# Second experts' down products with the weights stationary, copied out and turned back per token

## The chip, the cores and the metric

The kernel runs on one core of a Trainium2 chip. Its time is device microseconds for one execution; the runs before gave 628.49 us as the median of three (626.14 to 630.59). The trace comes from one further execution, which took 630.66 us.

## The reference

The program is a small language model tower on 16 x 128 tokens: a token layer with four MLP levels (width 128), an attention layer with a fast-weight recurrence (8 heads of 32), a first expert layer (8 experts, two chosen per sequence), a second attention layer, and a second expert layer (8 experts, two chosen per token). The change touches the last of these, and by one condition the first expert layer. Cut to what matters, the second expert layer is:

```
logits = xn @ Wr + br                       # xn: normalised x, 64 wide; 8 experts
top_vals, top_idx = top_k(logits, 2)
w_full = scatter(softmax(top_vals))         # 2 of 8 weights per token are not zero
for e in range(8):
    h = gelu(xn @ W1[e] + b1[e])            # 64 -> 128
    y_e = h @ W2[e] + b2[e]                 # 128 -> 64
    y = y + y_e * w_full[..., e, None]
return x + y
```

All eight experts are computed for every token, and the weights pick afterwards. All arithmetic is in float32.

## The kernel before

Five queues run by orders written out by hand: TensorE, VectorE, ScalarE, GpSimd and the DMA queue of SyncE. Each takes its instructions strictly in the order written, and waits on semaphores where it needs another engine's work. In the expert layers a "token" t is a block of 128 tokens (16 blocks), and four blocks make a chunk of 512 columns (c = 0 to 3). `x = 4 * k + c` numbers the chunks of both expert layers (k = 0, 1).

The steps of the second expert layer (k = 1), for one chunk:

- `turn_x` (L1567): four TensorE transposes of the normalised input into one PSUM bank. ScalarE's `experts` (L1054) copies it out with the norm's scale and bias.
- `expert_up` (L1583): for each expert one product of 512 columns with a contraction of 64 rows. Experts of even and odd number use different halves of the rows of the array. The result, 128 x 512, fills a PSUM bank; `expert_bank` (L367) names it. ScalarE's `expert_gelus` (L1067) takes it out through gelu into `G2`, of which there are two, for chunks of even and odd number.
- `expert_down` (L1617): for each block of 128 tokens eight products, one per expert. The stationary operand is the gelu block (128 x 128), the moving one the expert's weights (128 x 64). All eight fill one bank with tokens on the partitions and (expert, output) along the row (L1635). Banks 4 and 5 take turns.
- VectorE's `weigh` (L2503) multiplies that bank by the token's eight router weights into one of four buffers `ytmp`. GpSimd (L827 to L835) adds up the experts of two blocks in three halving additions and adds the sum to `H`; the last pair is done by VectorE (L2538 to L2543). SyncE sends `H` out in five transfers.

Beside it run the router of the second layer (`router`, `router_read`, `beaten_by`, `half_gaps`, `router_tanh`, `router_weights`), in two halves of eight blocks, and the experts' bias: the router's weights are turned (`turn_weights` L1814), saved by ScalarE (`save_weights` L1184) and multiplied by the biases (`second_bias` L1820, bank 7), and VectorE adds the result to `H` (`add_bias` L2497).

The order on TensorE around the change is L1830 to L1867, on ScalarE L1194 to L1211, on VectorE L2512 to L2543. On TensorE all down products of a chunk stand in few blocks: those of chunk 0 between the ups of chunk 1, those of chunk 1 between the ups of chunks 2 and 3, those of chunks 2 and 3 one after the other at the end. An up product waits for the gelu that freed its bank (`i >= 6`, L1588); four banks are in use.

The first expert layer (k = 0) has the same `expert_up`. In its chunk 0 experts 4 and 5 write to banks 4 and 5, which nothing else holds. Its down products have the router's weights multiplied into the expert weights, which stand still, 64 wide, while 128 gelu columns move; the experts of even and odd number write the two halves of the output rows (L1632). Its router runs on TensorE, VectorE and ScalarE between the first ups (L1603 to L1653); VectorE's copy L2358 takes the spread weights from bank 7 and releases GpSimd and ScalarE's copy L1086, behind which gelus 4 to 7 of chunk 0 stand.

Of the kernel before, what the change touches and what calls it, by code (L numbers as in the profile page):

```python
# [12 lines left out]
P = 128  # L13


T = 16
# [3 lines left out]
D = 64  # L20
# [4 lines left out]
CH = 4  # L25
# [112 lines left out]
def build(nc, a):  # L138
# [9 lines left out]
    with ExitStack() as ctx:  # L148
# [38 lines left out]
        def col(name, k=0, parts=P):  # L187
# [71 lines left out]
        G2 = [b.rearrange("p (e n) -> p e n", e=E) for b in (FT[:, 4096:8192], G[:].rearrange("p g n -> p (g n)"))]  # L259
        w2w = FT[:, 8704:12288].rearrange("p (k e d) -> p k e d", k=NW, e=E)  # L260
        ytmp = KKf[:, 0:2048].rearrange("p (k e d) -> p k e d", k=4, e=E)
        b2x = [b.rearrange("p (t d) -> p t d", t=T) for b in (XS[:, 2048:3072], SX[:, 0:1024])]
# [48 lines left out]
            held_saved held_T h_T query_row query_p query_mm o_mm o_add  # L311
            y_saved y_mm b2x_ready x_norm mean_mm mean_ready logit_mm r_sub r_exp r_prob load_mm r_spread
            spread_mm w_ready wT_mm wT_ready bias_mm base_ready w2w_ready x_T x_xT x_up0 x_up1 x_gelu x_down y_read
            f1_norm f_affine m4_ready
# [523 lines left out]
        def _(act):  # L838
# [228 lines left out]
            def expert_gelus(k, c, e0=0, e1_=E):  # L1067
                x = NC * k + c
                for e in range(e0, e1_):
                    act.wait_ge(s[f"x_up{e % 2}"], (E * x + e) // 2 + 1)  # L1070
                    if e == 0 and x >= 2:
                        act.wait_ge(s["x_down"], CH * (x - 1))
# [5 lines left out]
            act.wait_ge(s["mean_mm"], 1)  # L1078
            act.activation(meanT[:], bank[7][0:D, 0:T], ACT.Copy, scale=1.0 / P).then_inc(s["mean_ready"], 1)
# [123 lines left out]
            experts(1, 2)  # L1203
            expert_gelus(1, 1, 4, 6)
            save_weights(0)
            expert_gelus(1, 1, 6, E)
            experts(1, 3)
            expert_gelus(1, 2)
            router_tanh(1)
            save_weights(1)  # L1210
            expert_gelus(1, 3)  # L1211

        @block.tensor
        def _(pe):
# [342 lines left out]
            def means(c):  # L1557

                pe.wait_ge(s["x_norm"], c + 1)
                for t in range(CH * c, CH * c + CH):  # L1560
                    last = mm(bank[7][0:D, t:t + 1], XN[:, t, :], ones[:, 0:1], start=True, stop=True)
                if c == NC - 1:
                    last.then_inc(s["mean_mm"], 1)

# [40 lines left out]
            pe.wait_ge(s["mean_ready"], 1)  # L1605
            mm(bank[7][0:T, 64:64 + E], meanT[:], wr[0][0:D], start=True, stop=True).then_inc(s["logit_mm"], 1)
# [3 lines left out]
            mm(bank[7][0:T, 96:96 + E], ones[0:T, 0:T], rout[0:T, 0, :], start=True, stop=True).then_inc(s["load_mm"], 1)  # L1610
            turn_x(0, 1)
# [40 lines left out]
            mm(bank[7][:, 128:256], ones[0:T, :], spread, start=True, stop=True)  # L1652
            mm(bank[7][:, 256:384], spread, ones[0:T, :], start=True, stop=True).then_inc(s["spread_mm"], 1)  # L1653
            expert_up(0, 0, 6, E)
# [149 lines left out]

# [40 lines left out]
            expert_up(1, 1, 0, 4)  # L1845
            pe.wait_ge(s["d_add"], NC)
            pe.wait_ge(s["e_norm"], 3)
# [12 lines left out]
            expert_up(1, 2, 2, E)  # L1860
            expert_down(1, 1)
            turn_weights(1)
            expert_up(1, 3, 0, 4)
            second_bias(1)
            expert_up(1, 3, 4, E)
            expert_down(1, 2)
            expert_down(1, 3)  # L1867

        @block.vector
        def _(dve):  # L1870
# [439 lines left out]
            def small_softmax(x, j, out):  # L2310
# [15 lines left out]
            CAPACITY = float(-(-N * 5 // (4 * E)))  # L2326
            dve.wait_ge(s["logit_mm"], 1)
# [3 lines left out]
            dve.wait_ge(s["load_mm"], 1)  # L2331
            sc = rout[0:T, 4, :]
# [23 lines left out]
               mul).then_inc(s["r_spread"], 1)  # L2356
            dve.wait_ge(s["spread_mm"], 1)
            dve.tensor_copy(wts[:].rearrange("p t e -> p (t e)"), bank[7][:, 128:256]).then_inc(s["w_ready"], 1)  # L2358
# [144 lines left out]
            def weigh(c, j0=0, j1=CH):  # L2503

                for t in range(CH * c + j0, CH * c + j1):
                    dve.wait_ge(s["x_down"], T + t + 1)
                    if t >= 4:
                        dve.wait_ge(s["sum_done"], t // 2 - 1)
                    tt(ytmp[:, t % 4], bank[4 + t % 2][:].rearrange("p (e d) -> p e d", e=E),
                       wts[:, t, :].unsqueeze(2).broadcast_to([P, E, D]), mul).then_inc(s["y_read"], 1)  # L2510
# [12 lines left out]
            dve.wait_ge(s["w_ready"], 2)  # L2523
            weigh(0, 0, 3)
            add_bias(0)
            weigh(0, 3, CH)
            router_read(1)
            beaten = beaten_by(rout[:, 8:T, :], T // 2, P)
            weigh(1, 0, 1)
            half_gaps(1, beaten)  # L2530
            weigh(1, 1, 2)
            router_weights(1)
            weigh(1, 2, CH)
            dve.wait_ge(s["w_ready"], 3)
            add_bias(1)
            weigh(2)
            weigh(3)
# [64 lines left out]
```

## Time and profile before

| | |
|---|---|
| median of three runs | 628.49 us (626.14 to 630.59) |
| the profiled execution | 630.66 us, span 628.9 us, mean granted TensorE clock 0.977 |
| TensorE matmuls | 558.3 us busy (89%), 4546 records |
| VectorE | 428.8 us (68%) |
| ScalarE | 348.4 us (55%) |
| GpSimd | 346.8 us (55%) |
| second experts' down products (L1635) | 256 records, 29.6 us busy |

The span runs from the first to the last instruction of the profiled execution; some 1.8 us lie around it. A float32 product appears as two records, a transpose as one. The busy time of a matmul record includes the way through the array, so that records of one stream overlap; what they cost is read from the distance of their starts, or from the chain of waits, which follows the work that ended last. PEld is TensorE's weight load, which overlaps its products.

### The profile page before, as it was taken

To read this page: it belongs to the slowest core of one execution; us is meant where nothing else is said; L and a number is where in the kernel's file an instruction comes from. 1 tells how busy PE (TensorE), PEld (TensorE's weight loads), DVE (VectorE), ACT (ScalarE), POOL (GpSimd) and SP (SyncE) were. 2 spreads that over 40 slices of the span, in tenths; PEclk is the share of its full clock that TensorE was granted. 3 is DMA by queue.
4 is the path that set the end of the run, shared out by engine and by line. 5 is a ranking of instruction groups with operands and counts; after the bars stand their busy time and mean duration, and the time that the engine had idled before them with its cause. 6 is when DMAs were issued, how large, how long until landed. Compare 5 with 4: busy or idle time off the path is not lost.

```text
span 628.9 us, 12496 instructions
## 1 busy us (share of the span) xinstructions
PE 558.3 (89%) x4546; PEld 426.4 (68%) x4546; DVE 428.8 (68%) x1098; ACT 348.4 (55%) x908; POOL 346.8 (55%) x471
## 2 busy tenths in 40 slices
PE   7989999999987777878888888899999788989996
PEld 3556767778435665767777777786567677776785
DVE  4953563423878777899899888998313987766444
ACT  1264444444776664226688878760465668767530
POOL 1597653311450766779999899984266430001435
PEclk9999999999999989899999999999899999999999
DMA  8000000000000433200000000000000000000000
GB/s 278 14 1 1 2 0 1 1 1 2 0 2 2 80 76 64 78 1 1 2 1 1 1 2 1 2 1 2 0 1 2 2 1 1 2 2 2 9 9 17
DMA packets 10860, 10.43 MB, mean 17 GB/s; under 512 B 6000, under 2 KB 9840, under 8 KB 10544
## 3 DMA queue, kind: packets, MB, share of 16 engines
q1 hardware_dynamic: 8080, 7.54, 4.2%
q0 software_dynamic: 2144, 1.75, 1.5%
q8 instruction: 36, 0.59, 0.4%
q10 hardware_dynamic: 576, 0.35, 0.3%
q14 instruction: 24, 0.20, 0.1%
HBM read 5.77 MB, written 0.52 MB: 10 GB/s over the span
## 4 chain that ended last, share of the span: by engine, by line
PE 32%; DVE 15%; ACT 5%; POOL 5%; issue 3%; DVEq 0%; POOLq 0%; ACTq 0%
PE bank L1365 6%; PE bank L1594 5%; PE bank L1635 5%; DVE bank L2086 3%; PE bank L1539 3%; DVE features L2080 2%; POOL features L592 2%; PE bank L1681 2%; DVE features L2056 1%; DVE features L2409 1%; DVE RK L2405 1%; PE bank L1421 1%; POOL features L612 1%; PE bank L1632 1%; PE bank L1693 1%
## 5 line engine op out<-in xcount | busy, mean ns | idle before, releaser
L1365 PE MATMUL bank<-ident,features 128*128 128x128 f32 x604 | 78.1, 280 | 9.0 <-DVE features L2056 6.6
L1365 PEld LDWEIGHTS bank<-ident,features 128*128 128x128 f32 x604 | 69.2, 145 | 15.5 <-DVE features L2056 11.5
L864 ACT ACTIVATE G<-bank,cols 128x512 f32<-128x512 f32 x64 | 43.9, 686 | 53.0 <-PE bank L1266 53.0
L592 POOL TENSOR_TENSOR features<-UV,coefs 128x1024 f32<-128x1024 f32 (+3 forms) x36 | 59.7, 1681 | 2.9 <-DVE UV L2043 2.9
L1278 PE MATMUL bank<-weights,G 128*128 128x128 f32 x512 | 60.0, 275 | 0.0
L1266 PE MATMUL bank<-xs,weights 128*128 128x512 f32 x128 | 57.8, 594 | 0.9 <-ACT xs L855 0.9
L1278 PEld LDWEIGHTS bank<-weights,G 128*128 128x128 f32 x512 | 58.5, 192 | 0.0
L2056 DVE TENSOR_TENSOR features<-UV,bank 128x1024 f32<-128x1024 f32 (+3 forms) x68 | 55.7, 862 | 0.7 <-ACT bank L947 0.2
L392 POOL TENSOR_SCALAR rstd<-mv 128x4 f32<-128x4 f32 x8 | 1.6, 194 | 91.0 <-DVE mv L404 91.0
L954 ACT ACTIVATE xs<-UV,coefs 128x32 f32<-128x32 f32 x232 | 50.3, 308 | 0.0
L954 ACT ACTIVATE sx<-UV,coefs 128x32 f32<-128x32 f32 x200 | 43.4, 308 | 0.0
L1539 PE MATMUL bank<-RK,ident 128*128 128x256 f32 x186 | 43.4, 382 | 0.0
L1356 PE MATMUL bank<-features 32*128 32x136 f32 x768 | 34.6, 320 | 9.1 <-issue 3.6
L565 POOL TENSOR_TENSOR UV<-xs,rows 128x512 f32<-128x512 f32 x16 | 20.2, 1271 | 38.7 <-DVE xs L1945 38.6
L2086 DVE TENSOR_REDUCE bank<-features 128x32 f32<-128x1024 f32 (+3 forms) x40 | 41.0, 1051 | 0.0
L1266 PEld LDWEIGHTS bank<-xs,weights 128*128 128x128 f32 x128 | 23.1, 190 | 25.0 <-issue 22.7
L1356 PEld LDWEIGHTS bank<-features 32*128 32x128 f32 x768 | 30.1, 213 | 13.8 <-issue 6.4
L416 DVE TENSOR_SCALAR UV<-xs,mv,rstd 128x128 f32<-128x128 f32 x52 | 20.8, 463 | 24.9 <-POOL rstd L385 23.2
L1539 PEld LDWEIGHTS bank<-RK,ident 128*128 128x128 f32 x186 | 34.1, 191 | 3.9
L385 POOL TENSOR_TENSOR rstd<-rstd,neghalf 128x4 f32<-128x4 f32 x32 | 33.4, 1044 | 2.7
L1945 DVE TENSOR_TENSOR xs<-bank,UV 128x512 f32<-128x512 f32 x16 | 11.1, 691 | 33.3 <-PE bank L1278 31.2
L2080 DVE TENSOR_TENSOR features<-RK,bank 128x1024 f32<-128x1024 f32 (+3 forms) x32 | 32.2, 1008 | 0.7
(352 smaller groups left out, 1352.6 us busy)
## 6 DMA issues: line engine op xcount, KB each, us to landing
weights<-in_w SPq DMA_DIRECT2D x2, 1024.0 KB, 10.2
features<-in_tok SPq DMA_DIRECT2D x1, 768.0 KB, 5.8
weights<-in_ew SPq DMA_DIRECT2D x4, 128.0 KB, 3.4
weights<-in_ew SPq DMA_DIRECT2D x2, 256.0 KB, 3.2
coefs<-G POOLq DMA_DIRECT2D x16, 25.5 KB, 4.8
rows<-in_rows SPq DMA_DIRECT2D x1, 384.0 KB, 6.5
out_h<-H SPq DMA_DIRECT2D x3, 128.0 KB, 2.0
coefs<-G SPq DMA_DIRECT2D x14, 25.5 KB, 4.6
```

The lines of the kernel that those rows point to most:

```text
L385: pool.tensor_tensor(rstd[:, k, 0:n], rstd[:, k, 0:n], neghalf[:, 0:n], ALU.pow).then_inc(s["ln_rstd"], 1)
L592: pool.tensor_tensor(out, u, co, ALU.mult).then_inc(s["held_p"], 1)
L864: act.activation(G[:, 4 * (w % 2) + f, :], up_bank(f)[:], ACT.Gelu, bias=col("b1", 4 * i + f)).then_inc(s["tok_gelu"], 1)
L954: last = act.activation(own[t % 2][:, k, DH * h:DH * h + DH], UV[:, FIRST[t] + k, 0, DH * h:DH * h + DH], ACT.Copy, scale=C[:, t, 2 * NH + ...
L1266: mm(up_bank(f)[:], w1[:, i, P * f:P * f + P], xT[:, w % 2, :], start=True, stop=True).then_inc(s["tok_up"], 1)
L1278: last = mm(down_bank(w)[:, DT * j:DT * j + DT], G[:, 4 * (w % 2) + f, P * j:P * j + P], w2[:, i, f, :], start=(f == 0), stop=(f == 3))
L1356: last = mm(bank[4 * k + j][:, GB * SL * n:GB * SL * n + GB * SL], feat[left + k][x, g, 0:T].rearrange("p s b -> p (s b)"), feat[right + k ...
L1365: last = mm(out[:, P * k:P * k + P], x[:, P * k:P * k + P], ident[:], is_transpose=True, start=first and k == 0, stop=last_ and k == n - 1 ...
L1539: mm(bank[1][:, HB:2 * HB], ident[:], RK[:, 0, :], start=True, stop=True)
L2056: dve.tensor_tensor(out, u, co.unsqueeze(3).broadcast_to([P, R, NH, DH]), ALU.mult)\
L2080: ch(dve.tensor_tensor(PD[:, j, 0:R * HB].rearrange("p (r x) -> p r x", r=R), RK[:, r0:r1_, :], e.unsqueeze(1).broadcast_to([P, R, HB]), A ...
L2086: ch(dve.tensor_reduce(bankCR[:, r0:r1_, :], PD[:, j, 0:(r1_ - r0) * HB].rearrange("p (r h j) -> p r h j", r=r1_ - r0, h=NH), AX_X, ALU.add))
```

## The change

For the second experts the roles of the down product's operands are swapped. `pair_down(c, p)` takes two experts: their weights (128 x 64 each) stand in the two halves of the array's columns, and all 512 gelu columns of the chunk move. The result has (expert of the pair, output) on the partitions and the chunk's tokens along the row, in bank 4 or 5. It is copied to SBUF (`ypair`), pairs 0 and 2 by ScalarE, 1 and 3 by VectorE. `pair_back(c, j)` turns the four copies of a block of 128 tokens back with four TensorE transposes into bank 0 or 1, from where `weigh` reads it as before. There are 16 `pair_down`, 16 copies and 16 `pair_back`, 64 transposes in all, in place of 128 products.

Banks are dealt out anew: from chunk 1 on the ups use banks 2 and 3 only and wait for the gelu two before; chunks 2 and 3 are turned into bank 7, which they share with the bias. The three orders are written anew: on TensorE an up pair, a back and a down pair alternate for chunks 2 and 3. The condition of an up product's wait in the other cases goes from `i >= 6` to `i >= 4`. Four semaphores of the first router become one.

```diff
         def turn_bank(k, c):
-            return bank[6 if k == 0 else 2 + c if c < 2 else c % 2]
+            return bank[6 if k == 0 else (2, 3, 7, 7)[c]]
         def expert_bank(k, c, e):
             if k == 0 and c == 0 and e in (4, 5):
                 return bank[e]
-            low, high = ((2, 0), (3, 1)) if k == 0 or c >= 2 else ((2, 4), (3, 5)) if c == 0 else ((2, 1), (3, 7))
-            return bank[(high if e % 2 else low)[e // 2 % 2]]
+            if k == 0:
+                return bank[((3, 1) if e % 2 else (2, 0))[e // 2 % 2]]
+            return bank[2 + e % 2 + (2 if c == 0 and e // 2 % 2 else 0)]
...
+            def save_pair(c, p):
+                act.wait_ge(s["yp_mm"], CH * c + p + 1)
+                if c >= 2:
+                    act.wait_ge(s["x_down"], T + CH * (c - 1))
+                act.activation(ypair[c % 2][:, p, :], bank[4 + p % 2][:], ACT.Copy).then_inc(s["yp_act"], 1)
...
                 for e in range(e0, e1_):
                     i = E * x + e
-                    if i >= 6:
+                    if k and c:
+                        pe.wait_ge(s["x_gelu"], i - 1)
+                    elif i >= 4:
                         pe.wait_ge(s["x_gelu"], i - 3)
-                    if k == 1 and c == 1 and e == 2:
-                        pe.wait_ge(s["pos_saved"], NC // 2)
-                        pe.wait_ge(s["comb_done"], NC)
...
+            def pair_down(c, p):
+                x = NC + c
+                n = CH * c + p
+                pe.wait_ge(s["x_gelu"], E * x + (2 * p + 2 if c else E))
+                if n >= 2:
+                    pe.wait_ge(s["yp_dve" if p % 2 else "yp_act"], n // 2)
+                for h in range(2):
+                    last = mm(bank[4 + p % 2][D * h:D * h + D, :], ew2[1][:, 2 * p + h, :], G2[x % 2][:, 2 * p + h, :],
+                              start=True, stop=True)
+                last.then_inc(s["yp_mm"], 1)
+            def pair_back(c, j):
+                t = CH * c + j
+                pe.wait_ge(s["yp_act"], 2 * c + 2)
+                pe.wait_ge(s["yp_dve"], 2 * c + 2)
+                pe.wait_ge(s["y_read"], NC + max(0, t - 1))
+                if t < 2:
+                    pe.wait_ge(s["pos_saved"], NC // 2)
+                for p in range(CH):
+                    last = tr(bank[t % 2][:, P * p:P * p + P], ypair[c % 2][:, p, P * j:P * j + P], ident[:])
+                last.then_inc(s["x_down"], 1)
...
             def second_bias(h):
                 pe.wait_ge(s["wT_ready"], 2 + h)
-                pe.wait_ge(s["x_gelu"], E * (NC + 2))
-                if h:
-                    pe.wait_ge(s["base_ready"], 1)
+                pe.wait_ge(s["x_xT"], NC + 3 + h)
...
             turn_x(1, 2)
-            expert_down(1, 0, 0, 1)
-            expert_up(1, 1, 4, E)
+            pair_down(0, 0)
+            expert_up(1, 1, 4, 6)
             turn_weights(0)
-            expert_down(1, 0, 1, 3)
+            pair_down(0, 1)
+            expert_up(1, 1, 6, E)
+            pair_down(0, 2)
             second_bias(0)
-            expert_down(1, 0, 3, CH)
+            pair_down(0, 3)
             pe.wait_ge(s["e_norm"], 4)
+            pe.wait_ge(s["base_ready"], 1)
             turn_x(1, 3)
             router(2)
-            expert_up(1, 2, 0, 2)
-            router(3)
-            expert_up(1, 2, 2, E)
-            expert_down(1, 1)
-            turn_weights(1)
-            expert_up(1, 3, 0, 4)
-            second_bias(1)
-            expert_up(1, 3, 4, E)
-            expert_down(1, 2)
-            expert_down(1, 3)
+            for p in range(CH):
+                expert_up(1, 2, 2 * p, 2 * p + 2)
+                pair_back(0, p)
+                pair_down(1, p)
+                if p == 0:
+                    router(3)
+            for p in range(CH):
+                expert_up(1, 3, 2 * p, 2 * p + 2)
+                pair_back(1, p)
+                pair_down(2, p)
+                if p == 0:
+                    turn_weights(1)
+                if p == 1:
+                    second_bias(1)
+            for p in range(CH):
+                pair_back(2, p)
+                pair_down(3, p)
+            for p in range(CH):
+                pair_back(3, p)
```

ScalarE's order of chunks 2 and 3, and VectorE's from the first `weigh` on, after the change:

```diff
+            expert_gelus(1, 2, 0, 2)
+            save_pair(1, 0)
+            expert_gelus(1, 2, 2, 6)
             router_tanh(1)
+            save_pair(1, 2)
+            expert_gelus(1, 2, 6, E)
             save_weights(1)
+            expert_gelus(1, 3, 0, 2)
+            save_pair(2, 0)
+            expert_gelus(1, 3, 2, 6)
+            save_pair(2, 2)
+            expert_gelus(1, 3, 6, E)
+            save_pair(3, 0)
+            save_pair(3, 2)
...
+            save_pair(0, 1)
             add_bias(0)
+            save_pair(0, 3)
+            weigh(0, 0, 1)
             router_read(1)
             beaten = beaten_by(rout[:, 8:T, :], T // 2, P)
+            weigh(0, 1, 2)
+            save_pair(1, 1)
             half_gaps(1, beaten)
+            weigh(0, 2, 3)
+            weigh(0, 3, CH)
             router_weights(1)
+            save_pair(1, 3)
+            weigh(1, 0, 2)
+            save_pair(2, 1)
+            weigh(1, 2, 3)
             dve.wait_ge(s["w_ready"], 3)
             add_bias(1)
+            weigh(1, 3, CH)
+            save_pair(2, 3)
+            weigh(2, 0, 2)
+            save_pair(3, 1)
+            weigh(2, 2, CH)
+            save_pair(3, 3)
             weigh(3)
```

## Rows read from the trace of the kernel before

**Rows 1.** The page's first lines and shares of the chain of waits.
```profile
span 628.9 us, 12496 instructions
...
PE 32%; DVE 15%; ACT 5%; POOL 5%; issue 3%; DVEq 0%; POOLq 0%; ACTq 0%
```

**Rows 2.** Chain of waits, second experts: start us, us, engine, output, line, records.
```profile
576.52 1.92 PE bank L1594 x8
578.43 0.59 PE bank L1580 x4
...
586.42 1.05 PE bank L1826 x2
...
589.40 0.44 PE bank L1580 x4
589.85 0.79 PE bank L1810 x8
590.64 1.06 PE bank L1594 x4
591.70 0.99 PE bank L1810 x8
...
608.31 14.45 PE bank L1635 x128
...
622.78 0.70 DVE features L2509
...
625.47 0.29 DVE H L2543
```

**Rows 3.** Groups by line and shape, 560 us to the end.
```profile
L1635 PE MATMUL bank<-weights,features 128*128 128x64 f32 x128 | 14.9, 275 | 0.0
```

**Rows 4.** Busy time of each engine (and instructions), last stretch of products.
```profile
608.00:623.00 15.00, 14.74 (x129) 14.37 (x128) 5.06 (x8) 1.44 (x3) 8.58 (x12) 1.00 0.07 19
```

**Rows 5.** Timeline, second experts: start us, us, engine, line, operation, tiles.
```profile
568.25 1.13 PE L1594 MATMUL bank<-UV,weights 64*128 64x512 f32 x4
...
569.41 1.26 ACT L1073 ACTIVATE features<-bank,cols 128x512 f32<-128x512 f32 x2 [0.38 <-PE bank L1594]
...
588.35 2.60 POOL L832 TENSOR_TENSOR features<-features 128x512 f32<-128x512 f32 x3 [7.42 <-DVE H L2501]
...
601.21 2.61 POOL L832 TENSOR_TENSOR features<-features 128x512 f32<-128x512 f32 x3 [5.84 <-DVE features L2509]
...
604.31 2.60 POOL L832 TENSOR_TENSOR features<-features 128x512 f32<-128x512 f32 x3
```

**Rows 6.** Timeline of TensorE, a chunk of the first experts' down products.
```profile
468.75 3.71 PE L1632 MATMUL bank<-G,features 128*64 128x128 f32 x64
```

**Rows 7.** Groups by shape, whole span: copies of a full bank.
```profile
L1979 DVE COPY features<-bank 128x512 f32<-128x512 f32 x7 | 4.8, 683 | 1.6 <-PE bank L1344 1.6
...
L1149 ACT ACTIVATE UV<-bank 128x512 f32<-128x512 f32 x32 | 17.5, 611 | 2.1 <-PE bank L1693 2.0
```

**Rows 8.** Timeline, first experts, from the ups of chunk 0 on.
```profile
448.58 1.99 PE L1594 MATMUL bank<-sx,weights 64*128 64x512 f32 x8
...
450.50 0.66 PE L1580 MATMUL bank<-ident,UV 128*128 128x128 f32 x4
...
450.84 2.42 ACT L1073 ACTIVATE features<-bank,cols 128x512 f32<-128x512 f32 x4
...
451.54 0.48 PE L1652 MATMUL bank<-RK,ones 16*128 16x128 f32 x2 [0.39 <-DVE RK L2355]
...
452.29 0.29 DVE L2358 COPY RK<-bank 128x128 f32<-128x128 f32 x1 [0.80 <-PE bank L1653]
...
453.14 0.29 ACT L1086 ACTIVATE RK<-bank 128x128 f32<-128x128 f32 x1
```

**Rows 9.** Busy time by stretch; the third number from the end is the granted clock.
```profile
435.50:438.90 3.40, 3.40 (x37) 2.51 (x38) 1.79 (x12) 0.60 (x1) 1.26 (x2) 1.00 0.02 5
438.90:445.80 6.90, 6.63 (x24) 4.25 (x21) 2.23 (x11) 0.39 (x2) 1.16 (x2) 0.51 0.00 1
```

More of the change, by code:

```diff
@@ L260, in build @@
         w2w = FT[:, 8704:12288].rearrange("p (k e d) -> p k e d", k=NW, e=E)
+        ypair = [b.rearrange("p (k n) -> p k n", k=4) for b in (FT[:, 2048:4096], CF[:, 0:2048])]
         ytmp = KKf[:, 0:2048].rearrange("p (k e d) -> p k e d", k=4, e=E)
@@ L311, in build @@
             held_saved held_T h_T query_row query_p query_mm o_mm o_add
-            y_saved y_mm b2x_ready x_norm mean_mm mean_ready logit_mm r_sub r_exp r_prob load_mm r_spread
-            spread_mm w_ready wT_mm wT_ready bias_mm base_ready w2w_ready x_T x_xT x_up0 x_up1 x_gelu x_down y_read
+            y_saved y_mm b2x_ready x_norm mean_ready router_mm r_sub r_exp r_prob r_spread
+            w_ready wT_mm wT_ready bias_mm base_ready w2w_ready x_T x_xT x_up0 x_up1 x_gelu x_down yp_mm yp_act yp_dve y_read
             f1_norm f_affine m4_ready
@@ L1071, in expert_gelus @@
                     if e == 0 and x >= 2:
-                        act.wait_ge(s["x_down"], CH * (x - 1))
+                        act.wait_ge(s["x_down" if x < NC + 2 else "yp_mm"], CH * (x - 1) if x < NC + 2 else CH * (c - 1))
                     act.activation(G2[x % 2][:, e, :], expert_bank(k, c, e)[:], ACT.Gelu,
@@ L1077, in _ @@
             experts(0, 0)
-            act.wait_ge(s["mean_mm"], 1)
+            act.wait_ge(s["router_mm"], 1)
             act.activation(meanT[:], bank[7][0:D, 0:T], ACT.Copy, scale=1.0 / P).then_inc(s["mean_ready"], 1)
@@ L1203, in _ @@
             experts(1, 2)
+            save_pair(0, 0)
             expert_gelus(1, 1, 4, 6)
@@ L1206, in _ @@
             expert_gelus(1, 1, 6, E)
+            save_pair(0, 2)
             experts(1, 3)
-            expert_gelus(1, 2)
+            expert_gelus(1, 2, 0, 2)
+            save_pair(1, 0)
+            expert_gelus(1, 2, 2, 6)
             router_tanh(1)
+            save_pair(1, 2)
+            expert_gelus(1, 2, 6, E)
             save_weights(1)
-            expert_gelus(1, 3)
+            expert_gelus(1, 3, 0, 2)
[5 more added lines that the diff above has]
+            save_pair(3, 2)
         @block.tensor
@@ L1562, in means @@
                 if c == NC - 1:
-                    last.then_inc(s["mean_mm"], 1)
+                    last.then_inc(s["router_mm"], 1)
             tr = nc.tensor.transpose
@@ L1605, in _ @@
             pe.wait_ge(s["mean_ready"], 1)
-            mm(bank[7][0:T, 64:64 + E], meanT[:], wr[0][0:D], start=True, stop=True).then_inc(s["logit_mm"], 1)
+            mm(bank[7][0:T, 64:64 + E], meanT[:], wr[0][0:D], start=True, stop=True).then_inc(s["router_mm"], 1)
             for k in range(5):
@@ L1609, in _ @@
             pe.wait_ge(s["r_prob"], 1)
-            mm(bank[7][0:T, 96:96 + E], ones[0:T, 0:T], rout[0:T, 0, :], start=True, stop=True).then_inc(s["load_mm"], 1)
+            mm(bank[7][0:T, 96:96 + E], ones[0:T, 0:T], rout[0:T, 0, :], start=True, stop=True).then_inc(s["router_mm"], 1)
             turn_x(0, 1)
@@ L1652, in _ @@
             mm(bank[7][:, 128:256], ones[0:T, :], spread, start=True, stop=True)
-            mm(bank[7][:, 256:384], spread, ones[0:T, :], start=True, stop=True).then_inc(s["spread_mm"], 1)
+            mm(bank[7][:, 256:384], spread, ones[0:T, :], start=True, stop=True).then_inc(s["router_mm"], 1)
             expert_up(0, 0, 6, E)
@@ L2326, in _ @@
             CAPACITY = float(-(-N * 5 // (4 * E)))
-            dve.wait_ge(s["logit_mm"], 1)
+            dve.wait_ge(s["router_mm"], 2)
             ch(tt(rout[0:T, 3, :], bank[7][0:T, 64:64 + E], row("br0", parts=T), plus))
@@ L2330, in _ @@
             small_softmax(rout[0:T, 3, :], 0, rout[0:T, 0, :]).then_inc(s["r_prob"], 1)
-            dve.wait_ge(s["load_mm"], 1)
+            dve.wait_ge(s["router_mm"], 3)
             sc = rout[0:T, 4, :]
@@ L2356, in _ @@
                mul).then_inc(s["r_spread"], 1)
-            dve.wait_ge(s["spread_mm"], 1)
+            dve.wait_ge(s["router_mm"], 4)
             dve.tensor_copy(wts[:].rearrange("p t e -> p (t e)"), bank[7][:, 128:256]).then_inc(s["w_ready"], 1)
@@ L2508, in weigh @@
                         dve.wait_ge(s["sum_done"], t // 2 - 1)
-                    tt(ytmp[:, t % 4], bank[4 + t % 2][:].rearrange("p (e d) -> p e d", e=E),
+                    tt(ytmp[:, t % 4], bank[t % 2][:].rearrange("p (e d) -> p e d", e=E),
                        wts[:, t, :].unsqueeze(2).broadcast_to([P, E, D]), mul).then_inc(s["y_read"], 1)
@@ L2523, in _, with save_pair @@
             dve.wait_ge(s["w_ready"], 2)
-            weigh(0, 0, 3)
+            def save_pair(c, p):
+                dve.wait_ge(s["yp_mm"], CH * c + p + 1)
+                if c >= 2:
+                    dve.wait_ge(s["x_down"], T + CH * (c - 1))
+                dve.tensor_copy(ypair[c % 2][:, p, :], bank[4 + p % 2][:]).then_inc(s["yp_dve"], 1)
+            save_pair(0, 1)
             add_bias(0)
-            weigh(0, 3, CH)
+            save_pair(0, 3)
+            weigh(0, 0, 1)
             router_read(1)
             beaten = beaten_by(rout[:, 8:T, :], T // 2, P)
-            weigh(1, 0, 1)
+            weigh(0, 1, 2)
+            save_pair(1, 1)
             half_gaps(1, beaten)
-            weigh(1, 1, 2)
+            weigh(0, 2, 3)
+            weigh(0, 3, CH)
             router_weights(1)
-            weigh(1, 2, CH)
+            save_pair(1, 3)
+            weigh(1, 0, 2)
+            save_pair(2, 1)
+            weigh(1, 2, 3)
             dve.wait_ge(s["w_ready"], 3)
             add_bias(1)
-            weigh(2)
+            weigh(1, 3, CH)
[4 more added lines that the diff above has]
+            save_pair(3, 3)
             weigh(3)
```

1 line of the change is left out of this document (added).

## The prediction

> **What bounds the kernel now.** I read the page's shares first, then the chain of waits backwards from the end, then the timeline of the two stretches that the diff touches. The page has TensorE busy for most of the span and first in the chain [rows 1]. The chain shows the down products of the second experts on the path: at the end one unbroken run of 14.45 us for eight tokens, after which only a weighting, two reductions and an addition follow [rows 2]. The groups by shape give the whole of it: 128 records from each of the two gelu buffers [rows 3], of which the run of 128 shows 113 ns each, so sixteen tokens at 1.81 us: 28.9 us. In the last 15 us TensorE is busy 14.74 us, VectorE 5.06, ScalarE 1.44, GpSimd 8.58 [rows 4]: the last stage is TensorE's, and GpSimd is next.
>
> **The products.** Removed are the 28.9 us. Added are 16 pairs of 512-column products. In each pair the two write different halves of the 128 output rows. No row shows just that; the nearest does: the first experts' products, also 64 output rows per half, run 64 records of 128 columns in 3.71 us, 58 ns each, where a full-width transpose of 128 columns takes 110 (0.44 for four): the halves run side by side [rows 6]. 512 columns twice are then the 1.06 us that a pair of up products takes in the chain, its change of shape included; one after the other they would be 1.05 + 0.86 = 1.91 us [rows 2]. I take 1.06, since the nearest row has the same halves, and keep 1.91 for a rival. Streaming alone is 0.86, the difference between two pairs of ups (1.92) and one (1.06) [rows 2].
>
> The Trainium skill, "TensorEngine Tiling (Array Packing)", section "Performance Considerations", recommends exactly this swap of the two operands where the moving one has at most 64 columns, and allows it up to twice the speed; by that the 28.9 us would become 14.5 (an estimate from that page). The streams here agree (16 x 0.86 = 13.8), but the rule counts neither the turning back nor the changes of shape.
>
> **The turning back.** 64 transposes: four take 0.44 us where the shape stays, 0.59 after another [rows 2]. TensorE's order now alternates up pair, back, down pair, three shapes in a round: 1.06 + 0.58 + 1.06 = 2.70 us.
>
> **The copies.** Eight on ScalarE (0.61 us) and eight on VectorE (0.68) [rows 7]. Neither engine is full in this stretch, so they cost no busy time on the path; what counts is who waits. A copy starts about 1.1 us after its pair (the gelu starts 569.41 after ups at 568.25 [rows 5]), and the first token of a chunk can be turned only when all four copies are there.
>
> **Two banks instead of four** for the ups of chunks 1 to 3: up e waits for the gelu of e-2. In chunk 1 the ups 0 to 3 begin at 576.5 as before; the first gelu can end at 576.5 + 1.16 + 0.69 = 578.3, up 2 follows, up 3 a gelu step (0.6) later at 578.9 and streams 0.96 (the single product of 1.05 less 0.09 for the change before it). The turning of chunk 2 starts at 580.0 rather than 578.4: 1.6 late. From there: turn 0.58, six runs of pair and ups at 1.06, weights 0.4, bias 1.05, turn 0.59, router 0.79 = 9.8, so the ups of chunk 2 start at 589.7, 0.9 earlier than now (590.64) [rows 2].
>
> **From 589.7 to the end** TensorE has eight rounds (21.6), four times back and pair without ups (4 x 1.64 = 6.6), the last four backs (1.9), a router (1.0 [rows 2]), a turn of weights (0.3), a bias that shares the array with ups (0.85): 32.2, to 621.9. On top come waits that have no cover, because TensorE's order is fixed and nothing else is queued in front:
> - 0.4: the first ups of chunk 3 wait for the last gelu of chunk 2.
> - 1.6: ScalarE stands at saving the second router weights, which TensorE turns only after the first back and pair of that round; the up is done at 602.4, the turn at 604.8 (0.58 + 1.06 + 0.3 and the handovers), so gelu 0 of chunk 3 starts at 604.9, 2.5 us late; it ends at 605.6, where TensorE has been free for 1.0, and the other up of the two waits 0.6 more for gelu 1.
> - 1.8: twice (chunks 2 and 3, with no ups left between) the first back waits for VectorE's copy of the fourth pair: 1.12 + 0.09 + 0.69 + 0.05 less the 0.96 that the pair holds TensorE, 0.9 each.
> - 0.6: the last two backs wait for the reads of their banks.
>
> So the last back ends at 626.3 where the last product now ends at 622.76. The tail behind it is as now (622.78 to 625.76 [rows 2]): **+3.5 us**. GpSimd is right behind: the first pair of weighted tokens is there only at 597.6 (now 588.35), since the second token is weighted after VectorE's router comparison, which needs the router product behind the first round (593.4) and takes some 3.5 us; a pair of tokens takes 3.1 us (601.21 to 604.31) [rows 5], and the seventh ends at 628.7, half a microsecond before the last addition at 629.3. A faster TensorE would soon meet it.
>
> **A wait in the first experts.** The rewritten condition lets an up from the fifth on wait for the gelu four before it, in chunk 0 of the first experts too; now that begins with the seventh. Ups 4 and 5 of that chunk have banks of their own and start before any gelu (the run of eight records at 448.58 holds ups 2 to 5). After the change up 4 waits for gelu 0, 450.84 + 0.69, and up 5 for gelu 1, 0.6 later: 452.15. It streams 0.96, to 453.1; behind it on TensorE's queue stand the turn of chunk 2 (now 450.50) and the spread of the router weights (now 451.54), whose copy on VectorE is at 452.29 [rows 8]. The turn starts at 453.2, the spread at 453.7, and the copy, 0.75 behind as now, at 454.45 rather than 452.29. ScalarE's copy at 453.14 waits for it and goes to 454.76; gelus 4 to 7, the next ups and the first down products are queued behind. 0.54 of the 2.16 was slack under the first four gelus: **+1.6 us**, and from there to the second experts each step waits for the one before.
>
> **The sum.** +1.6 + 3.5 = +5.1 on the profiled execution's own 630.66 us (span 628.9 and 1.8 around it) is 635.8. That execution lies 2.2 above the median of the three runs, 628.49; on the median it is 633.6, and 0.4 is added because the steps take each handover at its shortest: 634.0. Renamed semaphores cost nothing; the output transfers follow the sums as now.
>
> **Rivals.**
> 1. *The clock falls at the new wait* (slower). For: TensorE's granted clock went from 1.00 (2.4 GHz) in 435.5 to 438.9 to 0.51 (1.2 GHz) in 438.9 to 445.8, after a stretch filled with small transposes and single columns and no long gap [rows 9]; after the change TensorE stands idle from 449.5 to 451.6 and then runs single ups on half the array. Against: now the stretch around 450 keeps its clock. The rest of up 5, the turn, the spread and two ups (some 2 us, not all on the path) would take twice as long until it rises: +1.4, 635.4. It decides as soon as the clock falls before the spread is done.
> 2. *The halves don't run side by side* (slower): 16 x 0.85 = 13.6 more, 647.6. Against it is [rows 6]; for it only that no row has 512 columns in this form.
> 3. *The swap pays* (faster): if changes of shape and the waits are covered, 16 x (0.86 + 0.44) = 20.8 stands against 28.9: -8.1, with +1.6 it is -6.5 and 622.0. For: the last stage is TensorE's alone [rows 4]. Against: the waits stand in a fixed order. It is also what the Trainium skill's swap rule, on the page named above, leads to.
> 4. *The wait in the first experts is covered* by work that I took for serial: 3.5 + 0.4, 632.4.
>
> **How the numbers follow.** A measurement of this kernel can tell about 1%, 6.3 us: faster is under 622.2, slower over 634.8. Forecast 0.50, at 634 with 2 us of error either way (same 0.34, slower 0.16); clock 0.24 (same 0.09, slower 0.15); halves 0.08, all slower; the swap pays 0.07, all faster; covered 0.11 (same 0.10, slower 0.01). Together faster 0.07, same 0.53, slower 0.40. The range 629 to 640 takes in the forecast with its error, the clock and the covered wait, and leaves out the swap, the halves and a little at either edge.
>
> **What would show it.** Right: no 64-column products at the end, pairs at about 1.06 us, an idle TensorE near 450 and the spread's copy near 454.4; gaps before the first backs of chunks 2 and 3 of some 0.9; the last GpSimd sum within a microsecond of the last addition. Wrong: pairs near 1.9 (rival 2), or fewer gaps than listed and a last back before 622 (rival 3), or the stretch before 490 as long as now (rival 4). The sum fails if ScalarE or VectorE turn out to be late at places where I have TensorE wait for nothing.

## The result and the profile after

The changed kernel takes 637.59 us (median of 4 runs, 636.51 to 639.78), the kernel before 627.50 (4 runs, 626.14 to 630.59). The ratio is 1.0149, with a 95% interval of 1.0114 to 1.0185: 1.5% slower, inside the predicted range, 3.6 us above the predicted 634.0, and not within 1%, the likeliest of the three outcomes. The profiled execution took 636.51 us, against 630.66.

On the page of the changed kernel, TensorE's share of the chain goes from 32% to 49%, GpSimd's from 5% to 10% [rows 1]. These shares don't measure the change: in the runs further down, the kernel before with one condition altered (b_cond4) has 52% and 10%, and the changed kernel with that condition put back (a_cond6) 28% and 6%. The page's first line and shares:

```profile
span 634.8 us, 12296 instructions
...
PE 49%; DVE 23%; POOL 10%; ACT 8%; issue 6%; DMA 2%; SPq 1%; DVEq 0%; POOLq 0%; ACTq 0%
```

**The first experts.** The timeline of the changed kernel from ScalarE's table load (the one ahead of the gelus) to the first down product, to be held against [rows 8]:

```profile
445.76 1.28 ACT L1075 ACT_TABLE_LOAD   x1
447.06 2.42 ACT L1075 ACTIVATE features<-bank,cols 128x512 f32<-128x512 f32 x4
...
447.80 2.09 PE L1614 MATMUL bank<-sx,weights 64*128 64x512 f32 x4 [1.88 <-ACT features L1075]
449.82 1.11 PE L1601 MATMUL bank<-ident,UV 128*128 128x128 f32 x4
450.86 0.79 PE L1672 MATMUL bank<-RK,ones 16*128 16x128 f32 x2
...
452.12 0.29 DVE L2413 COPY RK<-bank 128x128 f32<-128x128 f32 x1 [4.42 <-PE bank L1673]
...
456.76 1.97 PE L1652 MATMUL bank<-features 128*64 128x128 f32 x32
```

The same load in the kernel before:

```profile
449.55 1.28 ACT L1073 ACT_TABLE_LOAD   x1
```

The new wait is the 1.88 us ahead of ups 4 and 5. The spread's copy comes 6.36 us after the table load, where it came 2.74 after it (452.29 less 449.55). The turn, 0.66 us for four transposes in [rows 8], is 1.11 here. The busy time by stretch of the changed kernel shows the clock behind it (the last three numbers are the granted clock, the share of DMA and GB/s):

```profile
441.00:445.70 4.70, 4.70 (x25) 2.46 (x23) 2.70 (x17) 0.85 (x3) 0.00 (x0) 1.00 0.00 0
445.70:449.00 3.30, 1.42 (x6) 0.59 (x4) 1.72 (x9) 3.27 (x6) 0.00 (x0) 1.00 0.00 0
449.00:455.80 6.80, 6.80 (x20) 3.62 (x19) 1.04 (x4) 3.18 (x6) 3.31 (x4) 0.50 0.00 0
455.80:460.00 4.20, 4.20 (x43) 2.62 (x42) 0.00 (x0) 2.60 (x5) 4.20 (x5) 1.00 0.00 0
```

After a stretch in which TensorE was busy 1.42 of 3.30 us, it runs 6.8 us at 0.50, which is 1.2 GHz, and does there what the down products wait for.

**The second experts.** The groups by shape of the changed kernel show all 64 records of the pairs' products, in two rows of 32, in place of the 256 (two groups like that of [rows 3]):

```profile
L1831 PE MATMUL bank<-features,weights 128*64 128x512 f32 x32 | 8.6, 618 | 0.0
L1831 PE MATMUL bank<-G,weights 128*64 128x512 f32 x32 | 8.6, 618 | 0.0
```

The timeline of their rounds, an up pair (L1614), a back (L1844) and a down pair (L1831), with the waits that the prediction listed and the ends of GpSimd (L834, L837) and VectorE:

```profile
589.52 1.13 PE L1614 MATMUL bank<-UV,weights 64*128 64x512 f32 x4
...
597.47 2.62 POOL L834 TENSOR_TENSOR features<-features 128x512 f32<-128x512 f32 x3 [16.57 <-DVE features L2564]
...
601.66 1.61 PE L1614 MATMUL bank<-UV,weights 64*128 64x512 f32 x4 [0.47 <-ACT features L1075]
...
605.16 0.27 ACT L1189 ACTIVATE RK<-bank 64x128 f32<-64x128 f32 x1 [3.07 <-PE bank L1862]
...
606.29 1.61 PE L1614 MATMUL bank<-UV,weights 64*128 64x512 f32 x4 [1.17 <-ACT G L1075]
...
616.50 0.63 PE L1844 MATMUL bank<-ident,features 128*128 128x128 f32 x4 [0.84 <-issue]
617.06 1.08 PE L1831 MATMUL bank<-G,weights 128*64 128x512 f32 x4
...
619.53 2.63 POOL L834 TENSOR_TENSOR features<-features 128x512 f32<-128x512 f32 x3 [0.92 <-DVE features L2564]
...
623.77 1.06 PE L1844 MATMUL bank<-ident,coefs 128*128 128x128 f32 x8 [0.84 <-issue]
625.27 1.22 PE L1844 MATMUL bank<-ident,coefs 128*128 128x128 f32 x8 [0.44 <-DVE features L2564]
625.83 2.61 POOL L834 TENSOR_TENSOR features<-features 128x512 f32<-128x512 f32 x3
628.52 0.46 POOL L837 TENSOR_TENSOR H<-H,features 128x128 f32<-128x128 f32 x1
...
629.28 0.29 DVE L2616 TENSOR_TENSOR H<-H,xs 128x128 f32<-128x128 f32 x1
```

TensorE is through at 626.49 (before 622.74), VectorE's last addition ends at 629.57 (before 625.76). GpSimd's last sum ends at 628.97, and that one ended at 623.11 before: 5.86 later, not 3.8. Its row before:

```profile
622.66 0.45 POOL L835 TENSOR_TENSOR H<-H,features 128x128 f32<-128x128 f32 x1
```

Which of the two sets the end isn't in the chain of waits, which in both kernels ends in VectorE's last addition. It stands in the rows of the line that closes the program on each queue (DRAIN is the closing instruction), here of the changed kernel (queue, operation, count, ns, start of the first and the last in us):

```profile
L148 POOLq EVENT_SEMAPHORE  x2: 17/17/17, 634.6 to 634.7; - x2
...
L148 POOLq DRAIN  x1: 6058/6058/6058, 628.5 to 628.5; - x1
...
L148 SPq DRAIN  x1: 7/7/7, 631.4 to 631.4; - x1
```

And of the kernel before:

```profile
L148 POOLq EVENT_SEMAPHORE  x2: 17/17/17, 628.7 to 628.8; - x2
...
L148 POOLq DRAIN  x1: 6053/6053/6053, 622.6 to 622.6; - x1
...
L148 SPq DRAIN  x1: 7/7/7, 627.6 to 627.6; - x1
```

SyncE, which waits for the last output, closes 1.0 us ahead of GpSimd before (627.6 against 622.6 + 6.05) and 3.1 ahead after. GpSimd's closing starts with its last sum and takes 6.06 us, and the span ends 5.8 us after that sum in both kernels. So the length of the program is GpSimd's last sum plus 5.8.

The table below cuts the profiled executions at instructions that all kernels have: ScalarE's table load, the first down product of the first experts, the first gelu of the second experts, the end of GpSimd's last sum and of VectorE's last addition (us; the last column has the start and length of the stretches at 1.2 GHz between 435 and 460 and between 555 and 575). The runs below before and after are told under Experiments. In a_poollate, GpSimd's added addition stands in the place of its last sum; in b_best and a_fixed the last sum is GpSimd's sixth, not its seventh.

| kernel | table load to first down product | to first gelu of second experts | from there to GpSimd's last sum | from there to VectorE's last addition | GpSimd's last sum to the end | low stretches |
|---|---|---|---|---|---|---|
| before | 7.30 | 112.56 | 53.70 | 56.35 | 5.79 | 438.9 (6.8) |
| after | 11.00 | 112.61 | 59.60 | 60.20 | 5.80 | 449.0 (6.8) |
| a_cond6 | 7.31 | 114.15 | 59.60 | 60.20 | 5.79 | 439.1 (3.4), 562.0 (3.4) |
| b_cond4 | 12.34 | 113.09 | 53.71 | 56.36 | 5.80 | 447.5 (10.2) |
| a_fill | 9.02 | 114.22 | 59.60 | 60.20 | 5.80 | 563.6 (3.4) |
| a_turnw | 12.43 | 112.94 | 57.63 | 58.22 | 5.80 | 439.9 (3.4), 450.1 (10.2) |
| a_tail | 12.34 | 116.12 | 59.59 | 60.19 | 5.79 | 440.4 (3.4), 450.6 (10.2), 566.6 (6.8) |
| a_dvelate | 10.99 | 112.57 | 59.60 | 62.42 | 5.79 | 448.2 (6.8) |
| a_poollate | 10.99 | 112.56 | 60.91 | 61.06 | 5.97 | 438.6 (6.8), 452.3 (6.8) |
| b_best | 7.30 | 114.14 | 50.14 | 55.52 | 7.46 | 438.5 (3.4), 561.3 (3.4) |
| a_fixed | 7.31 | 114.13 | 54.54 | 59.56 | 7.10 | 438.8 (3.4), 561.6 (3.4) |

The change costs 3.7 us in the first experts and 5.9 at the end, 9.6 together; the medians differ by 10.1. The spans differ by 5.9 only, because the profiled execution of before reached the table load 3.8 us later (449.55 against 445.76): it was 0.8 behind at ScalarE's copy ahead of it (437.58 against 436.82), and lost the other 3.0 in its low stretch of [rows 9].

### The profile page after: what moved, and what is told of

Its sections match the earlier page's. It is cut to its first block, busy times and chain, and to the rows that moved or that the text cites. A ratio compares the mean times of both kernels' runs of the same rounds, so it can differ in the third digit from the quotient of the medians.

```text
span 634.8 us, 12296 instructions
## 1 busy us (share of the span) xinstructions
PE 553.5 (87%) x4418; PEld 400.8 (63%) x4418; DVE 434.6 (68%) x1106; ACT 353.8 (56%) x916; POOL 346.7 (55%) x471
## 4 chain that ended last, share of the span: by engine, by line
PE 49%; DVE 23%; POOL 10%; ACT 8%; issue 6%; DMA 2%; SPq 1%; DVEq 0%; POOLq 0%; ACTq 0%
PE bank L1299 8%; PE bank L1287 6%; PE bank L1386 6%; PE bank L1614 5%; DVE bank L2141 3%; PE bank L1377 3%; PE bank L1560 2%; DVE features L2135 2%; POOL features L594 2%; POOL rstd L387 2%; PE bank L1701 2%; DVE features L2111 2%; PE bank L1831 2%; DVE stats L403 1%; DVE features L2464 1%
## 5 line engine op out<-in xcount | busy, mean ns | idle before, releaser
L1386 PE MATMUL bank<-ident,features 128*128 128x128 f32 x604 | 76.6, 275 | 10.6 <-DVE features L2111 7.2
L1386 PEld LDWEIGHTS bank<-ident,features 128*128 128x128 f32 x604 | 66.7, 142 | 18.5 <-DVE features L2111 13.4
L1377 PE MATMUL bank<-features 32*128 32x136 f32 x768 | 32.3, 301 | 10.0 <-DVE weights L2059 3.7
L1377 PEld LDWEIGHTS bank<-features 32*128 32x128 f32 x768 | 27.5, 194 | 15.0 <-ACT weights L925 4.2
```

The costliest lines, as they stand in the source:

```text
L1377: last = mm(bank[4 * k + j][:, GB * SL * n:GB * SL * n + GB * SL], feat[left + k][x, g, 0:T].rearrange("p s b -> p (s b)"), feat[right + k ...
L1386: last = mm(out[:, P * k:P * k + P], x[:, P * k:P * k + P], ident[:], is_transpose=True, start=first and k == 0, stop=last_ and k == n - 1 ...
```

## Experiments

**The first experts' wait taken back (a_cond6) and put alone into the kernel before (b_cond4).** Edits, the first on the changed kernel, the second on the kernel before:

```diff
-                    elif i >= 4:
+                    elif i >= (4 if k else 6):
```

```diff
-                    if i >= 6:
+                    if i >= 4:
```

> The changed kernel with the first experts' condition put back (the fifth and sixth up of their first chunk wait for no gelu). Theory: the wait cost 1.6 us and a clock at 1.2 GHz behind it some 2 more, so that from ScalarE's table load (445.76 in the changed kernel) to the first down product of the first experts it takes 7.3 us again, as before the change, instead of 11.0; the second experts' stretch stays as changed (59.6 us from their first gelu to GpSimd's last sum); time 5.9 us over the kernel before, ratio 1.009. Rival: the clock fell for another reason and the wait was covered: 10 to 11 us from the table load to the first down product, ratio 1.015.

> The kernel before with nothing but the new condition of the first experts (the fifth and sixth up of their first chunk wait for the gelu four before). Theory: table load to first down product 9 us (clock stays at 2.4 GHz) to 11 us (it falls), instead of 7.3; the second experts unchanged at 53.7 us from first gelu to GpSimd's last sum; time 1.6 to 3.7 us longer, ratio 1.003 to 1.006. Rival, covered wait: 7.3 us and ratio 1.000.

Measured: a_cond6 634.78 us (median of 9), ratio to before 1.0084 (1.0045 to 1.0123); b_cond4 632.21, ratio 1.0064 (1.0039 to 1.0088). On the 628.89 us of before in these runs that is +5.3 for the second experts alone and +4.0 for the wait alone, with the clock behind it; together 9.3, where the whole change costs 9.4 by its ratio and 9.6 by the cuts. The two parts add up, within intervals of some 2.5 and 1.5 us either way. The timeline of b_cond4, with the same wait of 1.88 us at the same place:

```profile
445.54 1.28 ACT L1073 ACT_TABLE_LOAD   x1
...
447.57 2.65 PE L1594 MATMUL bank<-sx,weights 64*128 64x512 f32 x4 [1.88 <-ACT features L1073]
...
457.88 1.97 PE L1632 MATMUL bank<-features 128*64 128x128 f32 x32
```

Its busy time in the stretch that follows the wait:

```profile
447.50:457.70 10.20, 10.13 (x24) 4.95 (x24) 1.04 (x4) 5.72 (x11) 4.88 (x5) 0.50 0.00 0
```

The clock falls here too, for 10.2 us, and the stretch takes 12.34 us in place of 7.30. In a_cond6 TensorE has no such wait, and the stretch is back at 7.31.

**The wait kept, TensorE given work in it (a_fill).** Four products that nobody reads stand ahead of ups 4 and 5 of the changed kernel:

```diff
-            expert_up(0, 0, 2, 6)
+            expert_up(0, 0, 2, 4)
+            for k in range(4):
+                mm(bank[5][:, 0:HB], ident[:], RK[:, 0, :], start=True, stop=True)
+            expert_up(0, 0, 4, 6)
```

> The changed kernel with four filling products of 256 columns (into a bank that nothing reads) on TensorE where it waits for gelu 0 in the first experts. Theory: the clock at 1.2 GHz behind that wait is due to what TensorE does during it; with the filling it stays at 2.4 GHz, and from the table load to the first down product it takes 9.0 us (1.6 to 1.8 over the 7.3 of before) instead of 11.0. Rival: the clock falls all the same, or the wait alone costs the 3.7: 11.0.

Measured: 636.78 us, ratio 1.0128 (1.0099 to 1.0156). Its timeline:

```profile
447.98 1.28 ACT L1075 ACT_TABLE_LOAD   x1
448.06 1.99 PE L1635 MATMUL bank<-RK,ident 128*128 128x256 f32 x8
...
450.10 1.61 PE L1614 MATMUL bank<-sx,weights 64*128 64x512 f32 x4
...
457.00 1.97 PE L1655 MATMUL bank<-features 128*64 128x128 f32 x32
```

The table load comes 2.2 us later here than in the changed kernel, so that the low stretch there, 449.0 to 455.8, corresponds to 451.2 to 458.0. The busy time around it:

```profile
449.00:455.80 6.80, 6.45 (x26) 3.28 (x26) 1.84 (x8) 5.18 (x11) 2.45 (x3) 1.00 0.00 0
455.80:460.00 4.20, 4.20 (x43) 2.66 (x42) 0.00 (x0) 2.40 (x5) 4.20 (x5) 1.00 0.01 4
```

The clock stays at 1.00, and the stretch takes 9.02 us: the wait itself costs 1.7, and the fall behind it 2.0 more in the changed kernel (11.00), 3.3 in b_cond4 (12.34). In the whole time the gain does not show: the interval takes in the changed kernel's 1.0149, and this profiled execution has a low stretch at 563.6, which costs it 1.6 us between the first down product and the second experts (114.22 against 112.61).

**The order around the second router (a_turnw).** The turn of the router weights goes ahead of the first ups of chunk 3, so that ScalarE isn't kept waiting for it:

```diff
+            turn_weights(1)
             for p in range(CH):
                 expert_up(1, 3, 2 * p, 2 * p + 2)
                 pair_back(1, p)
                 pair_down(2, p)
-                if p == 0:
-                    turn_weights(1)
```

> The changed kernel with the second turn of router weights moved ahead of the first ups of chunk 3 on TensorE. Theory: ScalarE no longer stands at saving them, gelu 0 of chunk 3 starts some 2 us earlier, and the wait of the next two ups goes; GpSimd's last sum ends 57.7 us after the first gelu of the second experts instead of 59.6; time 1.9 us less than the changed kernel, ratio to the kernel before 1.012. Rival: GpSimd's own pace from its first pair sets the end: 59.6 as now, ratio 1.015.

Measured: 637.75 us, ratio 1.0137 (1.0111 to 1.0164). From the first gelu to GpSimd's last sum it takes 57.63 us, 1.97 less than the changed kernel. The whole time doesn't settle it: the interval takes in the expected 1.012 and the changed kernel's 1.0149, and the profiled execution had the longer low stretch in the first experts (12.43 us).

**Which engine's end counts (a_tail, a_dvelate, a_poollate).** In a_tail each down pair of chunk 3 goes ahead of the back of chunk 2. In a_dvelate VectorE does its last two reductions twice. In a_poollate GpSimd does one more addition on a buffer that nobody reads any more, after its last sum. Each of the three ran once:

```diff
             for p in range(CH):
-                pair_back(2, p)
                 pair_down(3, p)
+                pair_back(2, p)
```

```diff
-            for t in (T - 2, T - 1):
+            for t in (T - 2, T - 1, T - 2, T - 1):
+                ch.settle()
```

```diff
                 pool.tensor_tensor(h, h, y[:, :, 0], ALU.add).then_inc(s["sum_done"], 1)
+            pool.wait_ge(s["sum_done"], T // 2 - 1)
+            ch(pool.tensor_tensor(y[:, :, 0:4], y[:, :, 0:4], y[:, :, 4:8], ALU.add))
+            ch.settle()
```

> The changed kernel with the order of the last two chunks turned: the pair of chunk 3 stands ahead of the back of chunk 2, so that TensorE has work where it waits for VectorE's copy. Theory: GpSimd, at 3.1 us for a pair of tokens, is the bound there: TensorE's last back is 0.4 us earlier, GpSimd's last sum stays within 0.1 of 59.6 us after the first gelu of the second experts, and the span with it. Rival, TensorE's waits are the bound: both 0.4 to 0.9 earlier.

> The changed kernel with VectorE's two last reductions done twice, 2 us more ahead of its last addition. Theory: the end of the program hangs on GpSimd's last sum, 5.8 us before the end of the span, so the last addition and the last output transfer move 2 us later and the span (from the first gelu of the second experts) stays at 65.4 us. Rival, the last output sets the end: 67.4.

> The changed kernel with one addition more on GpSimd after its last sum (1.27 us, on a buffer that nobody reads any more; nobody waits for it). Theory: the span ends 5.8 us after GpSimd's last instruction, so from the first gelu of the second experts it takes 1.3 us more, 66.7. Rival, the last output sets the end: 65.4 as now.

Measured: 643.46, 635.68 and 641.45 us, beside 626.57 of the kernel before. What tells them apart is the way from the first gelu of the second experts to the end of the span, 65.40 us in the changed kernel (59.60 + 5.80). First a_dvelate, its last instructions:

```profile
626.33 4.17 DVE L2614 TENSOR_REDUCE xs<-features 128x64 f32<-128x512 f32 x4
627.55 0.45 POOL L837 TENSOR_TENSOR H<-H,features 128x128 f32<-128x128 f32 x1
...
630.53 0.29 DVE L2617 TENSOR_TENSOR H<-H,xs 128x128 f32<-128x128 f32 x1
```

Its addition comes 2.2 us later (62.42 from the first gelu, not 60.20), and the end doesn't move: 65.39 (59.60 + 5.79). SyncE is still done 0.9 us ahead of GpSimd's closing. Then a_poollate, its last instructions:

```profile
631.95 0.45 POOL L837 TENSOR_TENSOR H<-H,features 128x128 f32<-128x128 f32 x1
...
632.48 1.26 POOL L839 TENSOR_TENSOR features<-features 128x512 f32<-128x512 f32 x1
632.71 1.18 DVE L2619 TENSOR_TENSOR H<-H,xs 128x128 f32<-128x128 f32 x1
```

Its closing rows:

```profile
L148 POOLq DRAIN  x1: 5540/5540/5540, 633.9 to 633.9; - x1
...
L148 SPq DRAIN  x1: 7/7/7, 635.7 to 635.7; - x1
```

One addition more on GpSimd, 1.26 us, and the end is at 66.88 (60.91 + 5.97), 1.48 later. VectorE's last addition is late here too, by 0.86 (61.06, not 60.20): it takes 1.18 us beside GpSimd's extra addition, where it takes 0.29 in the changed kernel. That doesn't set the end, as SyncE is done 3.7 ahead of GpSimd's closing. In a_tail TensorE ends 0.43 us sooner, counted from the first gelu (56.69 against 57.12), and GpSimd's last sum stays where it was, 59.59, as expected. Its long whole time is from elsewhere: 12.34 us in the first experts, and 116.12 up to the second with 6.8 us at the low clock.

**What the findings are worth together (b_best, a_fixed).** b_best is the kernel before, with GpSimd's last pair of sums given to VectorE, which is busy 5.06 of 15 us there [rows 4]; the last two transfers wait for VectorE's additions:

```diff
-            for p in range(T // 2 - 1):
+            for p in range(T // 2 - 2):
                 pool.wait_ge(s["y_read"], NC + 2 * p + 2)
...
+            weigh(3, 0, 1)
+            reduce_own(T - 4)
+            weigh(3, 1, 2)
+            reduce_own(T - 3)
+            ch.settle()
+            tt(H[:, T - 4:T - 2, :], H[:, T - 4:T - 2, :], YB[1][:, T - 4:T - 2, :], plus).then_inc(s["out_done"], 1)
+            weigh(3, 2, 3)
+            reduce_own(T - 2)
+            weigh(3, 3, CH)
+            reduce_own(T - 1)
```

These lines take the place of `weigh(3)` and the two reductions behind it; `reduce_own(t)` is VectorE's reduction of a block that the kernel before has for the last two. a_fixed is the changed kernel with a_cond6, a_turnw, a_tail and the same step.

> The kernel before, with the seventh pair of tokens taken from GpSimd to VectorE, whose reductions stand in the gaps between its last weightings. Theory: GpSimd ends with its sixth sum, 3.6 us earlier, so that its closing no longer sets the end; VectorE's last addition is 0.8 us earlier (one reduction instead of two behind the last weighting), and the output transfer then ends the program: span 1.5 to 1.8 us shorter, ratio 0.997. Rival, GpSimd's end is of no account: 0.8 us shorter through VectorE alone, ratio 0.999.

> The changed kernel with four mends: the first experts' old condition, the turn of router weights ahead of the ups of chunk 3, pairs ahead of backs in the last two chunks, and the seventh pair of tokens on VectorE. Theory: -3.7 in the first experts, -1.9 by the turn, -1.5 at the end as the output of VectorE's last addition takes GpSimd's place: 2 to 4 us over the kernel before, ratio 1.003 to 1.006, so the swap doesn't pay even then. Rival: without its mishaps the swap gives back the 8 us of TensorE time: ratio under 0.995.

Measured: b_best 626.37 us (median of 12), ratio 0.9961 (0.9934 to 0.9988), the fastest of all kernels here; a_fixed 630.18, ratio 1.0029 (0.9998 to 1.0060). VectorE's last addition in b_best:

```profile
622.74 0.29 DVE L2554 TENSOR_TENSOR H<-H,xs 128x128 f32<-128x128 f32 x1
```

Its closing rows:

```profile
L148 POOLq DRAIN  x1: 6054/6054/6054, 617.2 to 617.2; - x1
...
L148 SPq DRAIN  x1: 7/7/7, 624.9 to 624.9; - x1
```

GpSimd's closing is over at 623.2 and covered; now the output's transfer sets the end, 2.07 us after the last addition (623.03 to 625.10). From the first gelu to the end b_best takes 57.6 us, before 59.5 (53.70 + 5.79), after 65.4, a_fixed 61.6. So the mends take 3.8 us off the changed kernel's second experts; the swap with the better order still stands 2.2 above the kernel before, and 4.0 above the kernel before with the same step on VectorE.

## Why the prediction came out as it did

The time came inside the range through the range's width: the two terms of the sum, +1.6 and +3.5, measured +3.7 (with the clock of rival 1) and +5.9.

**TensorE's path: right.** The ups of chunk 2 start at 589.52 (predicted 589.7). The down pairs take 1.01 us in the chain of waits and 1.08 as records (predicted 1.06): the halves do run side by side, and rival 2 falls. The listed waits are there: 0.47 at the first ups of chunk 3 (0.4), 1.17 and a stretched up pair, 1.61 for 1.06, behind the second router weights (1.6), 0.84 twice ahead of the first backs of chunks 2 and 3 (0.9 each, though the terms named for it make 0.99), 0.44 and more at the last backs (0.6). The pair behind the 0.47 is stretched to 1.61 too. In the chain of waits it hangs on VectorE's second router half (593.27 to 600.18) and on ScalarE's tanh, copy and gelu behind it, work that the prediction counted for GpSimd's first pair but not there. TensorE ends 3.75 us later (predicted 3.5), the last addition at 629.57 (629.3).

**The step that failed** is the last one of the second experts: "The tail behind it is as now (622.78 to 625.76 [rows 2]): +3.5 us." It took the last addition and its transfer for what ends the program. GpSimd's closing does, 1.0 us behind the transfer in the kernel before already. The prediction had GpSimd's own lateness nearly right: first pair 597.47 (597.6), seventh sum ending at 628.97 (628.7). It had only not read that the end follows from it: +5.9, not +3.5. a_dvelate (VectorE late, end unmoved) and a_poollate (GpSimd late, end moved) show that by themselves, and b_best from the other side. Why GpSimd was late is what the prediction said: it gets its first pair 9.1 us later than in [rows 5] and then has each pair no sooner than VectorE's weighting, until from 619.53 on it runs its last three pairs back to back in 9.44 us.

**The first experts: mechanism right, the clock mis-sized and under-weighted.** The wait was predicted at +1.6; a_fill, with the clock kept up, shows +1.7. That the clock falls behind it was rival 1, at a chance of 0.24 and a price of +1.4. It fell in each of the six profiled executions that have the wait without a_fill's products, and at this place in none of the other five; it costs 2.0 us where the low stretch is 6.8 long, 3.3 where it is 10.2. The price left out the ups and gelus that follow the spread: in the changed kernel 12 more up records take 4.82 us from 452.01, still on the path to the first down product. Rival 4, the covered wait, falls with a_cond6 and b_cond4.

**The swap doesn't pay (rival 3).** The pairs and backs take 16 x (1.01 + 0.59) = 25.6 us of TensorE's time in the chain against 28.9 for what they replace, so 3.3 us are saved on paper. TensorE's array is used less at the end: 8.21 busy of 13 us from 617 on, where it was 14.74 of 15 [rows 4]:

```profile
604.00:617.00 13.00, 10.99 (x47) 3.97 (x43) 4.65 (x7) 6.53 (x11) 4.89 (x8) 1.00 0.04 10
617.00:630.00 13.00, 8.21 (x46) 3.74 (x44) 8.88 (x13) 1.20 (x2) 10.16 (x15) 1.00 0.09 22
```

In the last stretch GpSimd is the busiest engine (10.16) and VectorE is ahead of TensorE (8.88). The rows suggest that the saving goes into round trips over the copies and into weighting that starts later; a_turnw shows 1.97 us of it, and no run prices the rest apart. The Trainium skill, "TensorEngine Tiling (Array Packing)", section "Key Properties", says that a change of tiling mode drains TensorE, and gives no size. The trace fits that, without showing what the time goes into: a round of up pair, back and down pair takes 1.06 + 0.59 + 1.01 = 2.66 us in the chain, where the streams alone, by the prediction's 0.86 and 0.44, would be 2.16.

**Open.** Low stretches of 3.4 us near 562 show in a_cond6, a_fill, b_best and a_fixed and not in before or after, and cost 1.5 to 1.6 us each; a_tail has one of 6.8 us at 566.6. As b_best has one, they don't come from the swap. What brings them was not settled, nor why the stretch in the first experts is 6.8 us in three executions and 10.2 in three. Neither was tried apart.

## What to carry to other kernels

Read the closing rows of every queue before deciding what ends a program: the last output's transfer was not it, and work given to an engine with a long closing costs its full length at the end, while the same work elsewhere may be free. A wait that is made a little stricter in shared code counts at every place that runs the code; here one condition, meant for the second experts, cost 4.0 of some 10 us in the first. When an operand swap saves stream time, count the round trip of its results through the other engines against it, and who gets their first piece later.

## What the runs showed of the hardware

GpSimd's closing takes 6.05 to 6.06 us from the start of its last sum (in a_poollate 5.54, from 0.2 after the end of its last addition), VectorE's 0.33 (1.22 in a_poollate), SyncE's 0.007. The span ends 5.8 us after GpSimd's last sum and, where that is covered, 2.07 us after VectorE's last addition (b_best); so in these kernels a GpSimd sum is free if it ends 3.7 us or more ahead of that addition (an estimate from these two numbers; it is 5.4 ahead in b_best, 2.65 in the kernel before). TensorE's clock fell to 1.2 GHz after a single wait of 1.88 us among products on half the array's rows, and stayed at 1.00 where four full-width products filled the wait. Whether the wait alone would have done it, without the half-height products, no run shows.
